# One-hot matrices of a group of edge tiles: one comparison and one product instead of four combined operations

## The reference, cut to what matters

```python
def _rgcn_conv(x, src, dst, etype, W, root, b):
    x_src = x[src]
    seg = dst * num_rel + etype
    sums = jax.ops.segment_sum(x_src, seg, num_segments=num_nodes * num_rel)
    cnt = jax.ops.segment_sum(jnp.ones(...), seg, num_segments=num_nodes * num_rel)
    mean = sums / jnp.maximum(cnt, 1.0)[:, None]
    mean = mean.reshape(num_nodes, num_rel, -1)
    out = jnp.einsum('nri,rio->no', mean, W)
    return out + x @ root + b
```

## Time and profile before

| | us |
|---|---|
| median of three runs | 3421.99 (3419.77 to 3424.31) |
| the profiled execution: its time | 3421.39 |
| the profiled execution: its span | 3419.5 |
| TensorE matmuls busy | 3174.5 (93%) |
| VectorE busy | 1773.6 (52%) |
| GpSimd busy | 1273.2 (37%) |
| aggregation, first layer | 650 to 1066 |
| aggregation, second layer | 1629 to 2048 |

### The profile page before, as it was taken

How to read it: one execution, slowest core, us unless ns; L and a number is a source line. 1 busy time by engine, 2 the same in 40 slices (tenths; PEclk the granted TensorE clock), 3 DMA queues, 4 the chain that set the end, 5 groups by cost and what they waited for, 6 DMA issues and landing times.

```text
span 3419.5 us, 64810 instructions
## 1 busy us (share of the span) xinstructions
PE 3174.5 (93%) x19556; PEld 2359.9 (69%) x19557; DVE 1773.6 (52%) x2941; ACT 762.8 (22%) x1086; POOL 1273.2 (37%) x1377
## 2 busy tenths in 40 slices
PE   6999999999997999999899989999886999999999
PEld 5788888777776888888677766776654555555555
DVE  7576666555555333333555552334586456455551
ACT  2211121000001212211000004444212543543540
POOL 2681000577772000002777761000420632652562
PEclk9999999999999999999999999999998999999999
DMA  5334334599994232321898882000330000000003
GB/s 149 101 106 149 118 116 137 171 306 307 306 306 140 87 120 94 118 95 63 319 307 307 303 287 78 14 28 14 88 95 24 20 1 19 19 1 19 19 28 95
DMA packets 101141, 433.58 MB, mean 127 GB/s; under 512 B 19648, under 2 KB 19971, under 8 KB 96818
## 3 DMA queue, kind: packets, MB, share of 16 engines
q0 software_dynamic: 55712, 266.87, 23.2%
q1 hardware_dynamic: 42593, 124.83, 11.6%
q10 hardware_dynamic: 2736, 40.50, 3.4%
HBM read 355.21 MB, written 76.88 MB: 126 GB/s over the span
## 4 chain that ended last, share of the span: by engine, by line
PE 71%; DVE 12%; issue 7%; DVEq 6%; ACT 1%; POOL 1%; DMA 1%; POOLq 0%; SPq 0%; ACTq 0%
PE PS L1466 26%; PE PS L1580 13%; PE PS L1776 5%; PE PS L1604 3%; PE PS L1711 3%; PE PS L1475 3%; DVE NM L1387 2%; PE PS L1612 2%; PE PS L1759 2%; PE PS L1760 2%; PE PS L1715 2%; PE PS L1649 2%; DVE HOT L1166 2%; PE PS L1633 2%; PE PS L1623 1%
## 5 line engine op out<-in xcount | busy, mean ns | idle before, releaser
L1466 PE MATMUL PS<-WHL,XT 128*125 (+1 forms) x3240 | 549.4, 329 | 7.0 <-DVE WHL L940 4.2
L1466 PE MATMUL PS<-WHL,HT 128*125 (+1 forms) x3240 | 531.8, 327 | 0.0
L1580 PE MATMUL PS<-GATA,HOT 128*125 128x384 f16 x2880 | 492.6, 328 | 37.0 <-issue 17.8
L1466 PEld LDWEIGHTS PS<-WHL,XT 128*125 (+1 forms) x3240 | 441.3, 138 | 92.7 <-issue 5.3
L1466 PEld LDWEIGHTS PS<-WHL,HT 128*125 (+1 forms) x3240 | 441.9, 137 | 84.2
L558 POOL DMA_INDIRECT GATA<-msg_table,SKEY x432 | 421.8, 976 | 163.0 <-issue 124.6
L1580 PEld LDWEIGHTS PS<-GATA,HOT 128*125 x2880 | 386.3, 137 | 114.5 <-issue 44.6
L1166 DVE SCALAR_TENSOR_TENSOR HOT<-NODE,DSTF,WHLO x720 | 297.0, 475 | 277.6 <-issue 277.6
L594 POOL TENSOR_TENSOR PL<-PF 125x500 bf16<-125x500 f32 (+1 forms) x360 | 320.6, 924 | 281.0 <-ACT PF L797 277.8
L1016 DVE SCALAR_TENSOR_TENSOR MSG<-PS,MSG 125x768 f16<-125x768 f32 x160 | 153.1, 957 | 360.3 <-ACT MSG L627 358.9
L627 ACT ACTIVATE MSG<-PS 125x768 f16<-125x768 f32 x160 | 129.6, 810 | 786.8 <-PE PS L1466 773.9
(11 more groups left out here) (254 smaller groups left out, 3898.6 us busy)
## 6 DMA issues: line engine op xcount, KB each, us to landing
msg_table<-MSG SPq DMA_DIRECT2D x160, 336.0 KB
WST<-in_wg_dram ACTq DMA_DIRECT2D x16, 2304.0 KB, 10.1
WST<-in_wf_dram SPq DMA_DIRECT2D x7, 1536.0 KB, 6.3
KROW<-key_rows POOLq DMA_DIRECT2D x54, 192.0 KB, 3.8
GATA<-msg_table,SKEY POOLq DMA_INDIRECT x432, 4.5
msg_table<-MSG SPq DMA_DIRECT2D x160, 39.0 KB
WST<-in_wm_dram SPq DMA_DIRECT2D x5, 1152.0 KB, 5.1
GATB<-msg_table,SKEY POOLq DMA_INDIRECT x216, 4.5
```

The lines of the kernel that those rows point to most:

```text
L1466: ins = pe.matmul(PS[0:ROWS, b0 + h, 0:HALF], X[:, xp, k, bass.ts(t, ROWS)], panel_part(slot, wp, k, h), start=k == 0 and xp + wp == 0, st ...
L1580: ins = pe.matmul(PS[0:ROWS, bass.ds(((n + (L + 1)) % 2) * 2 + h, 1), 0:HALF].rearrange("p a c -> p (a c)"), HOT[:, bass.ds((n % 2) * AT + ...
```

## The change

The four operations become two. A comparison over all four tiles writes a new f16 tile `SAME`, 128 by 4 by 125: 1 where the node is the edge's destination, else 0. After a drain a product of `SAME`, read twice by a broadcast, with the two weight parts writes all of the pass's `HOT`. `hot_made` is raised once a pass, so TensorE waits for the whole group's matrices ahead of each tile. The values in `HOT` are the same.

```diff
+        SAME = sb(gctx, "SAME", [128, AT, ROWS], f16)
...
-                        for k in range(AT):
-                            hot = HOT[:, bass.ds((n % 2) * AT + k, 1), :, :].rearrange("p a w c -> p (a w) c")
-                            node = NODE[:, bass.ds(b * ROWS, ROWS)].unsqueeze(1).broadcast_to([128, 2, ROWS])
-                            weight = WHLO[:, bass.ds(grp * AT + k, 1), :].rearrange("p a w -> p (a w)").unsqueeze(2).broadcast_to([128, 2, ROWS])
-                            v.scalar_tensor_tensor(hot, node, DSTF[:, bass.ds(grp * AT + k, 1)], weight, ALU.is_equal, ALU.mult).then_inc(S["hot_made"], 1)
+                        node = NODE[:, bass.ds(b * ROWS, ROWS)].unsqueeze(1).broadcast_to([128, AT, ROWS])
+                        edge = DSTF[:, bass.ds(grp * AT, AT)].unsqueeze(2).broadcast_to([128, AT, ROWS])
+                        v.tensor_tensor(SAME[:], node, edge, ALU.is_equal)
+                        v.drain()
+                        weight = WHLO[:, bass.ds(grp * AT, AT), :].unsqueeze(3).broadcast_to([128, AT, 2, ROWS])
+                        v.tensor_tensor(HOT[:, bass.ds((n % 2) * AT, AT), :, :], SAME[:].unsqueeze(2).broadcast_to([128, AT, 2, ROWS]), weight, ALU.mult).then_inc(S["hot_made"], 1)
...
-                                pe.wait_ge(S["hot_made"], n * AT + (k + 1))
+                                pe.wait_ge(S["hot_made"], n + 1)
```

## The result

The changed kernel takes 3478.66 us (median of 4 runs, 3474.22 to 3480.30) against 3420.88 (4 runs of the kernel before): ratio 1.0169, interval 1.0155 to 1.0183, slower. The forecast was 3484 with a range of 3440 to 3515; the growth is 57.8 us where 62.6 were summed. The profiled execution has a span of 3476.0 us, 56.5 more than in the earlier trace rows.

A forecast was written before the change was run, and what follows sets the result against it. Before, the gathers set the aggregation stage's length; after, the VectorE-TensorE ring would, at 9.84 us for two passes. Adding 32.1 us in the first layer and 30.5 in the second to 3421.4 gave 3484, range 3440 to 3515.

The forecast's parts named there:

- the ring: Aggregation over edges: VectorE and TensorE waiting on each other in turn; two passes grow from 8.22 to 9.84 us.
- the gap of the drain: VectorE, between comparison and product: idle time added, taken as 0.35 us, bounds 0.17 and 0.55.
- ROOT start to comparison: VectorE, from the start of the ROOT update to the new comparison: 2.70 us, one register step moved from 2.85.
- the slope of the earlier trace: 0.95 ns an element, from two broadcast comparisons in the earlier profile; gives the 1000-element product 1.19 us.
- the rival at twice that pace: Product on VectorE runs at two elements a cycle: ring 9.37 us, total 3443, still slower; chance 0.12.
- the clock rival: TensorE's clock falls because it idles in every pass: passes 6.83 us instead of 4.11, about 3720; chance 0.05.
- The dear end's ring: Upper bound of the sum: drain 0.55, product 1.32, no step moved; ring 10.31 us, total 3524.
- the gathers get their slots back late: GpSimd's gathers wait for buffer slots because the ring becomes the bound: 443 us for ninety passes against 415 for gathers.
- the old pace of 5.13 a group: GpSimd issues a group's four gathers in 5.13 us, 1.283 each; 81 groups make 415 us.
- GpSimd waiting for L1586 over and over: Sign that the forecast is right: GpSimd repeatedly waits for the small matmul that ends a group and frees its slots.
- GpSimd still waiting for nothing: Sign that the forecast is wrong: the consumers still don't hold GpSimd's gathers back.
- The rival with the hidden ring: Stage stays as long as its gathers: 3421 to 3424, or 3403 if fewer VectorE operations shorten gathers; chance 0.13.

The follow-up runs named there:

- the last run: Kernel after, second layer with before's four combined operations, TensorE waiting for the whole group and doing 8 of 24 matmuls a pass: 3432.02 us, kernel before 3422.36.
- The four-product run: Changed kernel with the product split into four of 250 elements, TensorE waiting tile by tile: 3672.85 us, 1.0043 against the kernel before.
- the first experiment: Kernel before plus an unread 1000-element product behind each ROOT update: 3649.78 against 3655.98 us, 0.9989.

## Why the number was right and its reason only in part

**Confirmed, term by term.** The comparison took 0.68 (0.71 used), the product 1.20 (1.19), the gap of the drain 0.33 (0.35), ROOT start to comparison 2.62 (2.70), the pass 4.11, the ring 9.73 (9.84). The product follows the slope of the earlier trace rows; the rival at twice that pace is out. With it goes the Trainium skill's figure for 16-bit `tensor_tensor` (VectorE: DVE Perf Modes, "The perf-mode tier table") for this form, with a broadcast weight. The clock stayed at 0.99 through TensorE's new pauses, so the clock rival is out too. It is not an empty one: with 8 matmuls a pass in the last run the stretch was granted 0.61. (The dear end's ring adds up to 10.32, not 10.31, which changes nothing.)

**The step that failed** is "the gathers get their slots back late", with its rider that the gathers come at the old pace of 5.13 a group: a longer gather was put at nothing. Of what was to show it, "GpSimd waiting for L1586 over and over" didn't come, and "GpSimd still waiting for nothing", listed under wrong, did. TensorE waited for HOT in 41 passes of 90, not in most. Its pass starts do alternate, in steps of 5.4 and 4.3 us around there, not 5.2 and 4.7. The timeline after:

```profile
818.38 0.16 PE L1588 MATMUL PS<-ZERO 128*1 128x1 bf16 x1
...
824.68 0.94 POOL L559 DMA_INDIRECT GATB<-msg_table,SKEY  x1 [0.30 <-issue]
```

The group whose last gather was issued at 811.97 is used up at 818.38, and GpSimd comes to refill its slots at 824.68. They have been free for 6.3 us. GpSimd goes at its own pace, and the pace has fallen since its gathers take 1083 ns: 4 x 1.387 = 5.55 us a group.

**Why the number came out all the same.** Two bounds rose to the same height. The ring needs 90 x 4.87 = 438 us for a layer; the 78 groups issued in the stage need 78 x 5.55 = 433, from a start 7 us later. TensorE ends only 6.3 us after the last gather, as before, and had little to spare.

The ring is no fiction: the profile's chain of waits over 650 to 1097 us runs through matmuls (46.1%), HOT (10.8%) and SAME (5.9%), and through gathers only from 952 to 961; but in the kernel before it has no gather either, so this chain can't tell the two bounds apart. The slots can. After the start of the stage 1.7 to 6.5 us pass from a group's L1588 to the first gather into its slots. The figure rises to about 6.1 each time TensorE has caught up, with a group's last tile used 0.2 to 1.0 us after it landed, and falls to about 2 when a group with two passes throws TensorE back. This comes again every 7 to 9 groups. So GpSimd is never held, TensorE is never more than a few us behind the landings, and the length of the stage is that of the gathers, with the ring just short of it. Had the gathers kept their 1.283, the ring would by the forecast's arithmetic have held them and the stage have ended at nearly the same time; no run on such a chip tried it. The forecast of +32.1 for the first layer (31.4 measured) is thus right in its ring, and lucky in that the bound which it left out lay no higher. For the second it was +30.5, and about 24 was measured; there the stretch from the 13th to the last gather, 1636.51 to 2040.35 before and 1670.97 to 2096.50 after, grew by 21.7 us, less than the ring's sum.

**The sign was safe** because both said slower. The rival with the hidden ring named the very row, the 1.17 us gather at 806.03, and drew the wrong conclusion from it: that fewer operations would take it away. What holds a gather is not how many operations there are but how much of an operation is still ahead when the gather begins. Four operations of 0.475 that follow each other at 0.39 let the gather go at the next boundary (all 140 that were held in the kernel before); one of 1.20 doesn't. The four-product run shows this most plainly: the same kernel with 250-element pieces has 1.056 where one piece has 1.2. Why two combined operations of 500 elements kept 33 gathers of 43 over their boundary is open.

On why, the Trainium skill (SBUF — State Buffer, "Who interferes with whom") says that a VectorE instruction with two inputs in SBUF contends with a GpSimd instruction that reads SBUF, through a shared read interface. The traces agree: 1.221 us with two inputs in SBUF, 0.948 with one in PSUM, and a gather reads its row numbers from SKEY in SBUF. They don't show that a gather holds VectorE in turn: 172 of the 180 products began in a running gather, and all took 1199 to 1203 ns, against 1199 on average in the run with SAME in PSUM. The rule spoke against this change, and the forecast didn't weigh it.

**What stays open.** How much of the 31 us each bound would hold by itself is shown from one side only, and by one profiled execution: with the ring lifted, 16.5 us remain. Why gathers begin in SAME and HOT at a worse moment when the ring is tight wasn't tried. So the hold is shown as a cause that works without the ring, and the ring stands so near the same height that it can't be ruled out as a second one. The cause of the slower chips is open.

## What to carry to other kernels

Where GpSimd issues gathers at a pace that bounds a stage, read their length, not only their waits: a mean of 977 ns where the shortest take 945 is a sign that another engine holds them. Merging VectorE operations with two inputs in SBUF into longer ones lengthens such gathers; short operations, or one input in PSUM, keep them short. Whether that saves time must be tried: on the chips where it was, both versions were 0.3 to 0.4% slower than the kernel before. And before a forecast moves the bound from one engine to another, it should ask whether the first one's own operations stay as long under the change.

## What the runs showed of the hardware that was not expected

- A gather begun in a VectorE operation with two tensor inputs in SBUF ends 0.82 us (median) after the operation, in every trace that has such operations; 0.945 us is its length otherwise. Begun in the operation's first 0.08 us it is mostly not held (23 gathers of the kernel before), and of two such operations back to back it was held to the end of the second in 33 cases of 43 in one run. Comparisons, products and combined operations do it alike; with one input in PSUM it is gone (0.948, 159 and 237 gathers).
- The same kernel takes 3421 us on some chips and 3641 to 3661 on others, at nearly the same clock over the whole (0.979 and, in the first experiment, 0.963), with single register steps of up to 0.72 us instead of 0.17. An edit's cost differs with it: 1.0169 on the one, 1.0032 on the other.
